# A retention layer and an FP4 feed-forward layer on one core: seventeen products for the down projection instead of eighteen, root chains over eight tiles, one small VectorE step given to GpSimd

## The reference, cut to what matters

```python
def fp4_quant_dequant(x):                       # BLOCK = 16, along the last axis
    xb = x.reshape(shape[:-1] + (shape[-1] // BLOCK, BLOCK))
    scale = jnp.max(jnp.abs(xb), axis=-1, keepdims=True) / 6.0
    scale = jnp.maximum(scale, jnp.float32(1e-12))
    xn = xb / scale
    idx = jnp.searchsorted(_MID, jnp.abs(xn))
    q = _GRID[idx] * jnp.sign(xn) * scale
    return q.reshape(shape)
def fp4_linear(x, w):
    return jnp.einsum('bsk,nk->bsn', fp4_quant_dequant(x), fp4_quant_dequant(w))
gate = fp4_linear(x, w_gate)                    # 256 -> 704
y = fp4_linear(x, w_up)                         # 256 -> 704
h = jax.nn.silu(gate) * y
return fp4_linear(h, w_down)                    # 704 -> 256
...
x = _layernorm(x + retention(x), axis=-1)
x = _layernorm(x + ffn(x), axis=-1)
```

## Time and profile before

| | us |
|---|---|
| median of 3 runs (584.76 to 586.46) | 584.79 |
| the profiled execution, its own time | 584.52 |
| span of the profiled execution | 582.7 |
| busy in the span: PE | 564.1 (97%) |
| busy in the span: DVE | 513.1 (88%) |
| busy in the span: ACT | 337.8 (58%) |
| busy in the span: POOL | 228.2 (39%) |

### The profile page before, as it was taken

The page is one execution under the profiler, slowest core; times in us unless marked ns, Lnnn a source line. Parts: engine busy times, 40 slices in busy tenths (PEclk is TensorE's granted clock), DMA queues, the critical chain, the costliest instruction groups (busy, mean ns, idle before and its releaser), DMA issues.

```text
span 582.7 us, 14053 instructions
## 1 busy us (share of the span) xinstructions
PE 564.1 (97%) x4432; PEld 485.7 (83%) x4432; DVE 513.1 (88%) x1283; ACT 337.8 (58%) x818; POOL 228.2 (39%) x260
## 2 busy tenths in 40 slices
PE   7999999999999999999999999999999999999984
PEld 3778888888888888888888788889999999999983
DVE  6567878988999998899899889999999999888896
ACT  4446766776676677667667644534454555455342
POOL 2211121534425344443534313565654655654420
PEclk9999999999999999999999999999999999999998
DMA  6601210110121011021001000000010100000002
GB/s 210 220 19 48 55 46 13 55 54 3 51 54 36 18 54 45 9 54 54 27 27 36 19 11 10 1 0 2 1 38 1 38 19 20 19 19 19 19 19 91
DMA packets 24983, 22.32 MB, mean 38 GB/s; under 512 B 2025, under 2 KB 21874, under 8 KB 24946
## 3 DMA queue, kind: packets, MB, share of 16 engines
q1 hardware_dynamic: 24130, 20.27, 11.5%
q10 hardware_dynamic: 816, 1.57, 0.8%
HBM read 17.63 MB, written 4.20 MB: 37 GB/s over the span
## 4 chain that ended last, share of the span: by engine, by line
PE 83%; DVE 7%; issue 4%; POOL 2%; DMA 2%; ACT 1%; ACTq 0%; DVEq 0%; POOLq 0%
PE wide_banks L1364 56%; PE wide_banks L1435 9%; PE wide_banks L1412 4%; PE wide_banks L1423 3%; PE wide_banks L1552 3%; PE turn L1461 3%; PE turn L1398 2%; PE wide_banks L1448 2%; DVE shared L854 1%; DVE shared L859 1%; POOL shared L1325 1%; PE turn L1561 1%; DMA pow_dram<-powers 1%; DVE shared L676 1%; DMA wgu_lo<-pow_dram 1%
## 5 line engine op out<-in xcount | busy, mean ns | idle before, releaser
L1330 POOL TENSOR_TENSOR shared<-shared,h_scale 128x704 f32<-128x704 bf16 x31 | 43.0, 1389 | 78.4 <-DVE shared L859 76.1
L1364 PE MATMUL wide_banks<-win_hi,x_hi 128*128 128x512 f32 x192 | 66.5, 428 | 2.2 <-DVE shared L676 1.5
L461 ACT ACTIVATE shared<-opened,rstd 128x64 f32<-128x64 f32 x240 | 63.5, 339 | 2.2 <-DVE rstd L772 2.1
L1435 PEld LDWEIGHTS wide_banks<-shared 128*128 128x128 f32 x512 | 62.0, 192 | 2.8
L558 ACT ACTIVATE shared<-wide_banks 128x512 f32<-128x512 f32 x64 | 29.6, 462 | 53.7 <-PE wide_banks L1364 53.3
L1435 PE MATMUL wide_banks<-shared 128*128 128x64 f32 x512 | 60.6, 271 | 0.0
L1364 PE MATMUL wide_banks<-wgu_hi,xq_hi 128*128 128x512 f32 (+1 forms) x192 | 59.7, 392 | 0.8 <-DVE xq_lo L1067 0.8
L1364 PE MATMUL wide_banks<-win_hi,x_lo 128*128 128x512 f32 x192 | 60.4, 396 | 0.0
L1364 PE MATMUL wide_banks<-win_lo,x_hi 128*128 128x512 f32 x192 | 60.4, 396 | 0.0
L427 ACT ACTIVATE shared<-shared 128x704 bf16<-128x704 f32 x32 | 25.3, 792 | 54.6 <-POOL shared L1325 52.2
L1364 PE MATMUL wide_banks<-wgu_lo,xq_hi 128*128 128x512 f32 (+1 forms) x192 | 56.6, 375 | 0.0
(11 more groups left out here) (146 smaller groups left out, 1440.5 us busy)
## 6 DMA issues: line engine op xcount, KB each, us to landing
xf<-in_x_feat SPq DMA_DIRECT2D x32, 128.0 KB, 2.3
tab<-in_tables SPq DMA_DIRECT2D x16, 256.0 KB, 2.7
xt<-in_x_tok SPq DMA_DIRECT2D x32, 128.0 KB, 2.1
out<-x SPq DMA_DIRECT2D x32, 128.0 KB, 1.7
x<-in_w_in ACTq DMA_DIRECT2D x3, 512.0 KB, 5.4
w<-in_w_gu SPq DMA_DIRECT2D x1, 1408.0 KB, 8.4
w<-in_w_down SPq DMA_DIRECT2D x1, 704.0 KB, 10.9
wgu_lo<-pow_dram SPq DMA_DIRECT2D x1, 576.0 KB, 4.5
```

What stands on the lines that cost most here:

```text
L461: last = act.activation(gated[:, b, cols], opened[:, b, cols], ACT.Copy, scale=rstd[:, b, 1 + k:2 + k])
L1330: pool.tensor_tensor(over_blocks(hq[:, b]), over_blocks(h_steps[:, b]), spread(h_fp4["scale"][:, b]), ALU.mult).then_inc(h_fp4["ready"], 1)
L1364: last = pe.matmul(dst, lhs, rhs, start=k == 0, stop=k == len(parts) - 1)
L1435: last = pe.matmul(mixed[:, r, DV * at:DV * (at + 1)], ret[:, slot(k)], vs[:, b, DV * k:DV * (k + 1)], start=False, stop=k >= HEADS - 2, s ...
```

## The change

Four edits, all in the feed-forward layer.

1. `down` leaves out the sixth product of hT_lo and wdown_hi. In its place VectorE writes the low part of h's last 64 columns into the 64 rows of `hT_hi` that repeated the fifth piece, and `wdown_hi` has there, instead of zeros, the weights of these columns once more (ScalarE copies them once; one VectorE memset is gone). So the sixth product of hT_hi and wdown_hi sums the high and the low part. `split_h` on VectorE becomes two instructions: 128x640, and 64x128 that reads partitions 64 to 127 of PSUM and SBUF and writes partitions 0 to 63.
2. GpSimd works out `h_scale`, behind `h_to_unit` and ahead of `rescale_x`; VectorE does it only for the last tile, and its `h_max` waits for the semaphore `h_scaled`.
3. The root chain of tiles 0 to 23 runs over eight tiles, in steps n = 12 to 15, 20 to 23 and 28 to 31; the last eight tiles keep two chains over four. The small buffers have eight columns.
4. ScalarE normalises two tiles a step, in four steps for each group of eight.

```diff
+        def chain_of(n):
+            first = n - n % QUAD - EIGHT - QUAD
+            if n - n % QUAD == QUAD:
+                return 0, range(QUAD - LAG, QUAD), None
+            if first >= 0 and first % EIGHT == 0 and n < TILES:
+                return 1 + first // EIGHT, range(EIGHT), first
+            return None
...
+                group, part = divmod(n - EIGHT - QUAD - 3, EIGHT)
+                if 0 <= group < 3 and part < QUAD and n < TILES:
+                    for t in range(2):
+                        norm_out(EIGHT * group + 2 * part + t, 1 + group)
...
             def h_max(n):
+                need(dve, h_scaled, n)
...
             def h_scale(n, b):
-                need(dve, h_fp4["ready"], n - 1)
                 dve.wait_ge(h_fp4["step"], H_STEPS * n + 1)
-                dve.tensor_scalar(h_fp4["scale"][:, b], h_fp4["amax"][:], 1.0 / FP4_MAX, SCALE_MIN, ALU.mult, ALU.max)
+                if n == TILES - 1:
+                    dve.wait_ge(h_fp4["ready"], n - 1)
+                    dve.tensor_scalar(h_fp4["scale"][:, b], h_fp4["amax"][:], 1.0 / FP4_MAX, SCALE_MIN, ALU.mult, ALU.max)
...
-                    for part in (wdown_hi, wdown_lo):
-                        last = dve.memset(part[0:F_OLD, c + 1].bitcast(F32), 0.0)
+                    last = dve.memset(wdown_lo[0:F_OLD, c + 1].bitcast(F32), 0.0)
...
-                dve.tensor_tensor(hT_lo[:, b], turned_h, hT_hi[:, b].bitcast(F32), ALU.subtract).then_inc(hT_lo_ready, 1)
+                dve.tensor_tensor(hT_lo[:, b, 0:FULL], turned_h[:, 0:FULL], hT_hi[:, b, 0:FULL].bitcast(F32), ALU.subtract)
+                dve.tensor_tensor(hT_hi[0:F_OLD, b, FULL:FC * P], turned_h[F_OLD:P, FULL:FC * P],
+                                  hT_hi[F_OLD:P, b, FULL:FC * P].bitcast(F32), ALU.subtract).then_inc(hT_lo_ready, 1)
...
+            def h_scale(n, b):
+                pool.wait_ge(h_fp4["step"], H_STEPS * n + 1)
+                need(pool, h_fp4["ready"], n - 1)
+                pool.tensor_scalar(h_fp4["scale"][:, b], h_fp4["amax"][:], 1.0 / FP4_MAX, SCALE_MIN, ALU.mult, ALU.max).then_inc(h_scaled, 1)
...
                 if valid(n - 1) and n < TILES:
                     h_to_unit(n - 1, 1 - b)
+                if valid(n - 1) and n < TILES:
+                    h_scale(n - 1, 1 - b)
                 if valid(n + 2):
                     rescale_x(n + 2, b)
...
-                                     ((hT_hi, wdown_hi), (hT_hi, wdown_lo), (hT_lo, wdown_hi)) for c in range(FC)]).then_inc(z_done, 1)
+                accumulate(z_of(b), [(t[:, b, P * c:P * (c + 1)], w[:, c]) for t, w, chunks in
+                                     ((hT_hi, wdown_hi, FC), (hT_hi, wdown_lo, FC), (hT_lo, wdown_hi, FC - 1))
+                                     for c in range(chunks)]).then_inc(z_done, 1)
```

More of the change, by code:

```diff
@@ L47 @@
 F_OLD = FC * P - FF
+FULL = (FC - 1) * P
 EPS = 1e-5
@@ L77 @@
 QUAD_STEPS = 12
+EIGHT = 2 * QUAD
 def slot(h):
@@ L190, in retention_ffn @@
         xq_lo = sb("xq_lo", [P, 2, KC, P], F32R)
-        stats2 = sb("stats2", [P, QUAD, 6])
-        moments2 = sb("moments2", [P, QUAD, 2])
-        quad = {k: sb(k + "2", [P, QUAD]) for k in ("var", "root", "rsq", "fine", "poly", "rstd", "shift")}
+        stats2 = sb("stats2", [P, EIGHT, 6])
+        moments2 = sb("moments2", [P, EIGHT, 2])
+        quad = {k: sb(k + "2", [P, EIGHT]) for k in ("var", "root", "rsq", "fine", "poly", "rstd", "shift")}
         ld_const, ld_proj, ld_w4, ld_decay = (sem(s) for s in ("ld_const", "ld_proj", "ld_w4", "ld_decay"))
@@ L545, in turn_weights @@
                 if old < BANK:
-                    act.activation(wdown_hi[F_OLD:P, c + 1], src[F_OLD:P, old:BANK], ACT.Copy).then_inc(w_hi_ready, 1)
+                    for rows in (slice(0, F_OLD), slice(F_OLD, P)):
+                        act.activation(wdown_hi[rows, c + 1], src[F_OLD:P, old:BANK], ACT.Copy).then_inc(w_hi_ready, 1)
             def split_xq(n, b):
@@ L563, in split_h, with norm_out @@
                 act.activation(hT_hi[:, b], turned_h, ACT.Copy).then_inc(hT_hi_ready, 1)
-            def norm_out(n, slot, ready):
-                act.wait_ge(quad_ready, QUAD + ready)
+            def norm_out(n, chain):
+                slot = n % EIGHT
+                act.wait_ge(quad_ready, QUAD * (chain + 1))
                 act.activation(x1[:, n], x1[:, n], ACT.Identity, bias=quad["shift"][:, slot:slot + 1], scale=quad["rstd"][:, slot:slot + 1]).then_inc(out_ready, 1)
@@ L600, in ffn_body @@
                     round_x_from({9: TILES, 15: TILES + 2, 21: TILES + 4}[n])
[L601 to L609, removed]
+                group, part = divmod(n - EIGHT - QUAD - 3, EIGHT)
+                if 0 <= group < 3 and part < QUAD and n < TILES:
+                    for t in range(2):
+                        norm_out(EIGHT * group + 2 * part + t, 1 + group)
+                if n == TILES:
+                    for t in range(TILES - 14, TILES - 12):
+                        norm_out(t, 3)
+                elif n == TILES + 1:
+                    for t in range(TILES - 12, TILES - EIGHT):
+                        norm_out(t, 3)
                 elif n == TILES + 2:
-                    for slot in range(QUAD):
-                        norm_out(TILES - 2 * QUAD + slot, slot, TILES - QUAD)
+                    for t in range(TILES - EIGHT, TILES - QUAD):
+                        norm_out(t, 4)
                 elif n == TILES + QUAD:
-                    for slot in (0, 1):
-                        norm_out(TILES - QUAD + slot, slot, TILES)
+                    for t in range(TILES - QUAD, TILES - 2):
+                        norm_out(t, 5)
             def finish(n):
@@ L949, in turn_weights @@
             def turn_weights(group):
-                dve.wait_ge(w_hi_ready, group + 1 + (group == W_GROUPS - 1))
+                dve.wait_ge(w_hi_ready, group + 1 + 2 * (group == W_GROUPS - 1))
                 if group < len(GU_GROUPS):
@@ L1039, in quad_root @@
                 dve.wait_ge(quad_step, done + 11)
-                if first > 0:
+                if first:
                     dve.wait_ge(out_ready, first)
@@ L1084, in ffn_body @@
                 out, quant = valid(n - 5), valid(n - 1)
-                first = n - 2 * QUAD - k
-                chain = first >= -QUAD and n < TILES
-                slots = range(QUAD) if first >= 0 else range(QUAD - LAG, QUAD)
-                done = QUAD_STEPS // QUAD * (first + QUAD)
+                chain = chain_of(n) is not None
+                if n >= TILES:
+                    number, slots, first = 4, range(QUAD), TILES - EIGHT
+                elif chain:
+                    number, slots, first = chain_of(n)
+                if chain or n >= TILES:
+                    done = QUAD_STEPS * number
                 if n > TILES:
@@ L1101, in ffn_body @@
                     if k == 0:
-                        quad_moments(n - 5 if first >= 0 else -1, slots)
+                        quad_moments(-1 if first is None else n - 5, slots)
                     elif k == 1:
@@ L1196, in last_bodies @@
                     add_out(n - 5, 1 - b)
[L1197 removed]
+                    out_stats(n - 5, (n - 5) % EIGHT)
                 if n == TILES + QUAD:
[L1199 removed]
+                    whole_chain(TILES - 1, done + QUAD_STEPS, range(QUAD, EIGHT), TILES - EIGHT)
                     for t in (TILES - 2, TILES - 1):
[L1201 removed]
+                        norm_last(t, t % EIGHT)
             def norm_last(n, slot):
[L1204 removed]
+                dve.wait_ge(quad_ready, QUAD * 6)
                 dve.tensor_scalar(x1[:, n], x1[:, n], quad["rstd"][:, slot:slot + 1], quad["shift"][:, slot:slot + 1],
```

18 lines of the change are left out of this document (7 added, 11 removed).

## The result

Side by side on one chip the changed kernel takes 589.67 us (median of 7, 588.65 to 591.43) and the kernel before 586.43 (7, 584.62 to 586.77). The ratio is 1.0075, with a 95% interval of 1.0060 to 1.0089: slower, by more than 0.3%, and outside the range that I gave. The profiled execution took 589.62 us with a span of 586.8 us; that of before had 584.52 and 582.7.

What follows compares the result with a forecast made beforehand. Bounds: VectorE to 389.91 us, TensorE for steps 6 to 31, VectorE in the tail. Gains of 1.89 us less 0.4 in the tail gave -1.5: 583.0 profiled, median 583.3; 8-in-10 range just under 581.4 to 585.6.

Steps and rivals of the forecast that it cites:

- h_scale on GpSimd: GpSimd's added operation delays xq and, in rounding steps, VectorE's L854: 0.20 us each, ends 0.09 and 0.41.
- the split pair: VectorE's split of h as two operations loses overlap when partitions change: +0.29 us, charged mainly in steps with late x pieces.
- TensorE's step: One product fewer saves 0.12 us a tile; where TensorE is the bound, its step becomes 6.74 us.
- the memset's 0.27: One memset leaves VectorE in n = 2, on the path: 0.27 us saved.
- it counts seven times up to step 18: GpSimd's h_scale delay counts in n = 4, 5, 10, 11, 16, 17 and at xq itself.
- h_scale off VectorE: VectorE's queue is freed of 0.11 us in each of 31 steps, ahead of the reciprocal.
- Eight aggregations: Chains over eight add 0.29 us in n = 12; chain-free steps 8 to 11 and 16 to 19 save about 0.55 and 0.3.
- After step 18: VectorE's waits for TensorE, up to 0.8 us a step, cover all additions; 13 more down products give -1.56 us.
- The tail: Pair costs 0.29 us once, some 0.2 at the last split of h; last product saves 0.12: +0.4.
- C: Rival: slower through GpSimd's h_scale; 0.41 us eats the gain, from 0.66 over 0.3% slower, at 0.73 587.0 us; chance 0.08.
- B: Rival: the two split operations overlap like any other pair (+0.02 us), VectorE stays ahead: -3.4 us, 581.4; chance 0.30.
- D: Rival: granted clock halves for the 34 last products after TensorE idles: net +2.6 us, 587.4; chance 0.06.

Runs made afterwards that it cites:

- the fifth experiment: Kernel before with the 17 products, both split operations working from partition 0 and ScalarE writing the copy on partitions 64 to 127: 583.05 us, ratio 0.9958.
- the fourth experiment: Changed kernel with h_scale put back on VectorE: 586.24 us, ratio 1.0020 against the kernel before.
- the 17 products alone: Kernel before with one product fewer and the split of h in two only; h_scale on VectorE, chains over four: ratio 1.0018.
- the seventh experiment: Changed kernel with GpSimd's h_scale moved behind rescale_x and the rounding, ahead of rescale_h: 585.41 us, ratio 0.9997 against the kernel before.
- the eleventh: Changed kernel with the split of h from partition 0 and nothing else; h_scale stays ahead of xq in GpSimd's queue: 585.83 us.
- the first four experiments: Kernel before with products and split, GpSimd's h_scale, or chains and normalising alone; changed kernel with h_scale on VectorE: 1.0018, 1.0027, 0.9997, 1.0020.
- the ninth kernel: Kernel before with 17 products, split from partition 0, chains over eight and normalising two a step; h_scale on VectorE: 583.42 us, ratio 0.9966.
- the third kernel: Kernel before with the chains over eight tiles and the normalising in four steps alone: ratio 0.9997.

## Why the prediction was wrong

The step that failed first is h_scale on GpSimd, in its price and still more in where I counted it. My terms for the move make R(18) 0.78 us earlier (18 x -0.11 + 6 x 0.20); against the kernel with h_scale on VectorE it came 2.27 later, and the time is 3.4 us longer. The second is what I charged for the split pair and the chains up to R(12): 0.66 us for a measured 1.57. I take the terms in turn.

**TensorE's step** was right: 6.74 us, 530.85 to 537.59 in the changed kernel.

```profile
530.85 0.38 PE L1589 MATMUL turn<-ident,xq 128*128 128x128 f32 x2
...
537.59 0.38 PE L1589 MATMUL turn<-ident,xq 128*128 128x128 f32 x2
```

**The split pair** was right in mechanism and size, +0.29, and the fifth experiment shows that the partitions are the reason. The Trainium skill's rule (VectorE: DVE Perf Modes, section "Two Vector instructions with no wait between them") held: the trace agrees with 0.01 and 0.04 us between the operations, and with overlap where the partitions stay. What I charged for it was too low. In the fourth experiment, with h_scale on VectorE, R(12) is 1.57 later than before, and my terms without h_scale's make +0.66. Of the difference 0.4 lie ahead of R(6), where I had the memset's 0.27 on the path; in the trace of the 17 products alone nothing of it shows by R(3) (-0.04 from R(1)). Between R(6) and R(12) the 17 products alone put 1.33 where I had charged 0.90, and the chains alone 0.04 where I had -0.26. By its ratio of 1.0018 this part alone made the kernel slower.

**h_scale on GpSimd** failed twice. The term "0.20" was mis-sized: it is 0.56 (operation 0.36, 0.08 ahead of it, 0.08 behind it, and 0.04 of overlap that was lost). I had extrapolated from the two-input forms in the earlier trace rows to a one-input form of another kind, and the upper end of 0.41 was too low as well. My estimate of 0.13 from the Trainium skill's cycle count (GPSIMD Engine Reference, section 3.1) was farther off. Worse was the step "it counts seven times up to step 18". I had asked who waits for GpSimd, and found xq and the roundings. I had not asked what VectorE does at the moment to which xq moves. In the earlier trace rows xq ends at 423.15, R + 2.48. With 0.56 more it lies beside x_scale, x_unit and x_exponent, which then take 0.33 us more each, and in the rounding steps beside L870. That is 0.27 us in each of eight steps, 2.16 of the 3.6 us that lie between the last reciprocals of the changed kernel and of the fourth experiment. The Trainium skill has the rule that I did not bring to this place (SBUF — State Buffer, section "SBUF: two separate sides"): a VectorE operation in a mode that uses two ports, or with two SBUF inputs while GpSimd's operation reads SBUF, and a GpSimd operation exclude each other for the whole of the one that came first. The trace agrees for the operations with two SBUF inputs: L870's 1.03, x_unit's 1.01, L875's 1.80 and, the other way round, GpSimd's rounding at 1.94. x_scale and x_exponent have one SBUF input and were lengthened all the same; they fit the rule only if they ran in such a mode, which no row here shows. That the place of xq and the roundings is the cause is shown by the seventh experiment: they got it back, h_scale stayed on GpSimd, and the loss was gone.

**h_scale off VectorE** gives 0.07 us a step and not 0.11 (L861 to L866 0.25, L844 to L850 0.32 with it).

**Eight aggregations** and the relief in steps without a chain: alone they changed nothing in the time (0.9997), but the relief was smaller and later than I had it: 0.39 by R(18), where I had 0.57, and none by R(12).

**After step 18** I let VectorE's slack cover everything. It had 0.8 us in single steps, but the steps n = 19 to 23, with late pieces and roundings, took it 6.70 to 7.25 us each, most of them above 6.74. From n = 18 to the last transpose of xq TensorE won 0.77 us, where I had 1.56 to the end of the down products.

**The tail** was forecast at +0.4. From R(32) to the last transpose of h it is 7.52 us in the changed kernel (565.97 to 573.49), 6.93 before: +0.59, and nearly all of it is the pair, which stands there twice on the path and not once. With h_scale on VectorE it is 7.88; 0.36 of that is a later L873, whose cause stays open.

**Rivals.** C, slower by GpSimd's h_scale, is what happened, at a chance of 0.08; its price was within what I had named (0.56 between 0.41 and 0.66), its count was not: 0.56 counted seven times would have added 2.5 us to my sum and made 585.8. B's pair exists where the partitions stay (0.92 us in the fifth experiment, 0.88 in B), but B's 581.4 us would not have come with it: the changed kernel with that pair took 585.83 (the eleventh), and only with h_scale moved back too 582.31. D did not come. The granted clock was low in the changed kernel a little later than before,

```profile
566.00:567.00 1.00, 0.00 (x0) 0.00 (x0) 0.96 (x2) 0.00 (x0) 0.00 (x0) 1.00 0.00 0
568.00:570.00 2.00, 1.49 (x7) 1.52 (x8) 1.85 (x10) 1.13 (x3) 0.00 (x0) 0.63 0.15 52
570.00:572.00 2.00, 2.00 (x12) 2.00 (x11) 1.79 (x3) 1.94 (x4) 0.00 (x0) 0.52 0.24 79
```

but it was 1.00 again from 573.4 to 580.0 us, when the last products ran, and from the last transpose of h to the end both kernels take 13.2 to 13.3 us (586.8 - 573.49, 582.7 - 569.46).

## What to carry to other kernels

When an operation goes to another engine's queue, the first question is not how long it takes but what stands behind it there, and then what the neighbours do at the time to which that is moved: here 0.36 us on an engine that idles more than half the time cost 3.4 us, and the same operation one or two places further back cost nothing. A small operation that starts on other partitions than those around it costs its neighbours' overlap, 0.23 us of 1.15; if an engine with room can do the move between partitions, let it. And price half-hidden costs together: alone the two edits cost 0.18 and 0.27% of this kernel, together (with the chains, which cost nothing) 0.75%.

## What the runs showed of the hardware

GpSimd lengthens some of VectorE's operations and not others. L1092 and the split, with one input from PSUM, kept 0.89 and 0.81 us beside GpSimd. So did the block maxima L854, a reduction with one input from SBUF: 0.88 at 414.48, beside L1356 from 414.40 to 415.79. L870, L875 and x_unit, with two inputs from SBUF, were lengthened, and so were x_scale and x_exponent, `tensor_scalar` with one. So the number of SBUF inputs alone does not decide it. Where two hold each other up, the one that comes second ends as if it had begun 0.13 to 0.15 us ahead of the other's end: 0.75 after it for an operation of 0.89, 0.55 for 0.68, 0.28 for 0.42, 0.04 for 0.17, and on GpSimd's side 1.15 for the 1.30 of the rounding (426.98 to 428.13).

The first 20 us differ from one execution to the next. The profiled execution of the 17 products alone reaches R(1) 1.7 us later than that of before (352.10 and 350.39), ahead of anything that the edit touches. Between 15 and 20 us, first before, then this kernel (columns as in the earlier trace rows):

```profile
15.00:20.00 5.00, 5.00 (x52) 3.51 (x50) 1.92 (x3) 1.39 (x3) 1.50 (x3) 1.00 0.90 270
```

```profile
15.00:20.00 5.00, 5.00 (x17) 3.43 (x16) 1.22 (x1) 0.63 (x2) 0.78 (x2) 0.66 0.96 300
```

The granted clock was 0.66 there instead of 1.00. The chains of eight alone show nearly the same, 1.8 us (352.23) at a mean clock of 0.91 in the first 20 us, and the times of the kernel before itself lie in two groups (584.4 to 585.1 and 586.2 to 586.7 us, 35 of them beside the first four experiments). The profiled execution of the ninth kernel does the same: R(1) at 352.39, granted clock 0.74 between 15 and 20 us (the third kernel: 0.77). The profiled executions of all other kernels had 1.00 there and R(1) at 350.4 to 351.1. The profiled executions of these three lie among the slowest of their kernels (588.13, 586.32 and 585.81 us). Where these traces are compared with others, the offset is taken off. What sets the clock there was not tried.
